# A fused RWKV layer and gated MLP on one core: the order of instructions in time mixing, at the head of the first unit and at stage heads is redone

## The chip, the cores and the metric

One Trainium2 chip, one core. The metric is the device time of one launch in microseconds (us), the median of several runs. All engines are told apart: TensorE (PE, its weight loads PEld), VectorE (DVE), ScalarE (ACT), GpSimd (POOL), and SyncE (SP), which here only issues DMAs. Each engine works through its own list of instructions in order; semaphores tie the lists together.

## The reference

```python
x  = x0 = (1, 2048, 512) tokens;  x = layernorm(x0)            # T = 2048, H = 512
h  = LN(x, ln1);  hh = shift(h)                                 # time mixing
k, v, r = ((h*m + hh*(1-m)) @ W.T for m, W in ((mk,Wk),(mv,Wv),(mr,Wr)))
wkv = (e1*0 + exp(ww-p)*v) / (e1*0 + exp(ww-p))                 # ww = tm_first + k, p = max(-1e38, ww)
x  = x + (sigmoid(r) * wkv) @ Wo.T
h  = LN(x, ln2);  hh = shift(h)                                 # channel mixing
kv = silu((h*cm_mk + hh*(1-cm_mk)) @ Wkey.T) @ Wval.T           # 512 -> 2048 -> 512
x  = x + sigmoid((h*cm_mr + hh*(1-cm_mr)) @ Wcr.T) * kv
x  = x0 + x                                                     # around the attention part
g, up = split(layernorm(x) @ w_gate_up.T);  x = x + (silu(g) * up) @ w_down.T   # 512 -> 2 x 2048 -> 512
```

## The kernel before

**Numbers.** Every matrix product is done in three passes: an operand is split into a high part (fp32r, rounded by an ACT copy) and a low part (the rest, a subtraction on POOL or DVE), and PE multiplies high by high, high by low, and low by high. `..._hi` names the ACT copy, `..._lo` the subtraction.

**Time mixing.** The 2048 tokens are four blocks `b` of 512. For each block PE transposes the normalised tokens into banks A0 to A3 (`norm1`), and ACT, DVE, ACT and POOL turn each of four tiles into an operand: `rest_of` (ACT, L731: the shifted part), `mix` (DVE, L1080 and L1082), `operand_hi` (ACT, L720), `operand_lo` (POOL, L1405). These tiles go through `made`, a ring of four, so a new `rest_of` waits for the POOL subtraction of the tile four places before it. PE then runs, in this order, `receptance(b)`, `output(b-1)`, `key(b)`, `value(b)`, each 48 matmuls of 128x512 on banks B0 to B3. A bank comes free when the sigmoid of the receptance was taken (`receptance_gate`, ACT L748), when DVE added the output to the residual (`output`, L1140), after the exponentials (`wkv_weight`) or after `gated_value` (DVE, L1128). Weights come by SP's DMAs into `landed` and are split by `matrix_hi` (ACT L715) and `matrix_lo` (POOL L1393 or DVE L1107).

**Channel mixing's preparation.** `norm2`, `mix("cr", b)` and `mix_ck(b)` make the operands; PE runs `channel_receptance(b)`; ACT takes its sigmoids (L799), which also free the banks. `x_added(b)` is a POOL DMA that adds the input onto the residual in place; SP then stores the block (`keep_x1`, L380), and after it, in SP's order, `keep_raw(1)`, `keep_gate(2)`, `load_quart(1)`, `keep_gate(3)`, `load_tall(0)`.

**Units.** The two MLPs run as 48 units of a seven-product scheme (Strassen's form) in four stages, starting at units 0, 8, 16 and 32. Units 0 to 15 are key units (0 to 7 and 8 to 15: two pairs of blocks), 16 to 47 gate units. The left operands of a unit come from `quart` (a 0.5 MB DMA, `load_quart`), completed by `sums(u)` on DVE (L1161 to L1166) and split by `unit_left_hi` (ACT L811, L814) and `unit_left_lo` (POOL L1426); the seven right operands of a stage (`combo`: B11, T3, T2, B21, T1, B22, T4) are made by `right_sums`, `make_t2`, `make_t4` (DVE L1203) and split by `combo_hi_of` (ACT L841) and `combo_lo_of` (DVE L1189). The second matmul's right operand is `right` (`unit_right_hi`, L824, and `unit_right_lo`, L1443). Each unit on PE is: products X(B11), V(T3), output tiles of the unit before (`some(0)`), Y(T2), X(B21), tiles, Y(T1) (which waits for `seed`, DVE L1266), tiles, Z(T4), Y(B22) (which waits for `sum_v`, DVE L1270), tiles. `norm3(j)`, at four units, transposes block j for the last MLP into the banks of the output tiles, and ACT copies them out (L880). Silu is taken at L855 and L867.

The order is written out by hand for each engine, in the four engine programs and in their `unit(u)`.

## Time and profile before

| | |
|---|---|
| median of 3 runs | 1101.29 us (1101.24 to 1101.83) |
| the profiled execution: its own time, and its span | 1100.64 us, 1098.8 us |
| PE busy, share of the span | 1060.4 us, 97% |
| DVE, ACT, POOL busy | 633.2, 485.9, 537.9 us |
| chain that ended last | PE 83%, DVE 8%, ACT 3%, POOL 3% |

The span runs from the first to the last instruction. Busy PE time counts a matmul from its start to its modelled end, so matmuls that run at half clock or overlap count as busy too; what is left open between the rows is idle time, and each idle stretch is put down to the instruction that released it.

### The profile page before, as it was taken

The page shows a single profiled execution, that of the slowest core. Times are in us where ns is not written, and L with a number is a line of the kernel's source. Part 1 is how long each engine was busy: PE and PEld are TensorE (multiplying, and loading weights), DVE is VectorE, ACT ScalarE, POOL GpSimd, SP SyncE. Part 2 cuts the span into 40 slices and gives each one's busy share as a digit, 9 for nine tenths or more (in the row PEclk, how much of TensorE's full clock was granted, in tenths as well). Part 3 has the DMA queues.
Part 4 walks back from the last instruction along what each step waited for, and adds up shares of the span by engine and source line. Part 5 has one row for each costly group of instructions (what it writes and reads, how often), then busy time and mean ns, then how long its engine had stood idle before and what let it go on. Part 6 is the DMA issues. An engine that isn't in the chain of part 4 may idle for free.

```text
span 1098.8 us, 13090 instructions
## 1 busy us (share of the span) xinstructions
PE 1060.4 (97%) x4704; PEld 871.4 (79%) x4704; DVE 633.2 (58%) x1106; ACT 485.9 (44%) x807; POOL 537.9 (49%) x451
## 2 busy tenths in 40 slices
PE   5979999999899999999999899999999999999998
PEld 4768888777688888888887788888887888888887
DVE  7866765685344447465449567675658434333334
ACT  6765676855533444433444433334335222222221
POOL 6483652733865553553535656654553323333322
PEclk9989999999999999999999999999999999999999
DMA  8000222257843442653232466575436463444422
GB/s 309 1 1 1 39 39 77 39 211 234 315 144 130 183 172 78 199 186 125 86 106 106 163 225 194 204 229 190 160 129 220 153 205 119 146 153 144 153 78 77
DMA packets 45233, 157.18 MB, mean 143 GB/s; under 512 B 4080, under 2 KB 4208, under 8 KB 40560
## 3 DMA queue, kind: packets, MB, share of 16 engines
q1 hardware_dynamic: 30000, 108.10, 28.1%
q0 software_dynamic: 15168, 48.24, 14.8%
q8 instruction: 37, 0.61, 0.2%
q14 instruction: 28, 0.23, 0.1%
HBM read 97.60 MB, written 58.72 MB: 142 GB/s over the span
## 4 chain that ended last, share of the span: by engine, by line
PE 83%; DVE 8%; ACT 3%; POOL 3%; issue 1%; DMA 1%; SPq 0%; ACTq 0%; DVEq 0%
PE bank L480 15%; PE bank L481 14%; PE bank L482 14%; PE bank L491 13%; PE bank L492 13%; PE bank L493 13%; DVE combo L1189 2%; POOL operand L1405 1%; POOL weights L1393 1%; DVE made L1080 1%; DVE weights L1107 1%; DMA tall_staged<-tall 1%; PE bank L638 1%; DVE resid L1215 1%; PE bank L548 0%
## 5 line engine op out<-in xcount | busy, mean ns | idle before, releaser
L1215 DVE TENSOR_TENSOR resid<-bank,resid 128x512 f32<-128x512 f32 x240 | 165.1, 690 | 243.5 <-PE bank L482 242.3
L491 PE MATMUL bank<-combo,left 128*128 128x512 f32 x672 | 262.8, 391 | 10.2 <-ACT made L855 3.3
L1448 POOL TENSOR_TENSOR inner<-made,inner 128x512 fp32r<-128x512 f32 x128 | 165.9, 1316 | 200.3 <-ACT inner L846 200.3
L493 PE MATMUL bank<-combo,left 128*128 128x512 f32 x672 | 262.0, 390 | 0.0
L492 PE MATMUL bank<-combo,left 128*128 128x512 f32 x672 | 262.0, 390 | 0.0
L480 PE MATMUL bank<-right,inner 128*128 128x512 f32 x512 | 200.0, 391 | 2.8 <-ACT raw L880 2.7
L482 PE MATMUL bank<-right,inner 128*128 128x512 f32 x512 | 199.2, 389 | 0.0
L481 PE MATMUL bank<-right,inner 128*128 128x512 f32 x512 | 199.2, 389 | 0.0
L1426 POOL TENSOR_TENSOR left<-quart,left 128x512 fp32r<-128x512 f32 x96 | 115.6, 1227 | 102.9 <-ACT left L811 63.3
L491 PEld LDWEIGHTS bank<-combo,left 128*128 128x128 f32 x672 | 126.4, 188 | 40.1 <-issue 7.7
L493 PEld LDWEIGHTS bank<-combo,left 128*128 128x128 f32 x672 | 126.4, 188 | 26.4
L492 PEld LDWEIGHTS bank<-combo,left 128*128 128x128 f32 x672 | 126.4, 188 | 25.8
L1443 POOL TENSOR_TENSOR right<-tall_staged,right 128x512 fp32r<-128x512 f32 x64 | 82.8, 1303 | 67.4 <-ACT right L824 67.4
L480 PEld LDWEIGHTS bank<-right,inner 128*128 128x128 f32 x512 | 96.2, 188 | 24.2 <-ACT raw L880 3.7
L482 PEld LDWEIGHTS bank<-right,inner 128*128 128x128 f32 x512 | 96.1, 188 | 20.1
L481 PEld LDWEIGHTS bank<-right,inner 128*128 128x128 f32 x512 | 96.3, 188 | 19.8
L1405 POOL TENSOR_TENSOR operand<-made,operand 128x512 fp32r<-128x512 f32 x64 | 84.9, 1424 | 44.2 <-ACT operand L720 44.2
L867 ACT ACTIVATE made<-bank 128x512 f32<-128x512 f32 x64 | 38.1, 595 | 153.9 <-PE bank L493 153.9
L1280 DVE TENSOR_TENSOR made<-bank,made 128x512 f32<-128x512 f32 x64 | 44.2, 691 | 61.7 <-ACT made L867 41.1
L846 ACT ACTIVATE inner<-made 128x512 fp32r<-128x512 f32 x128 | 77.2, 628 | 2.7 <-ACT made L855 0.4
L855 ACT ACTIVATE made<-bank 128x512 f32<-128x512 f32 x64 | 37.6, 587 | 83.8 <-PE bank L493 83.8
L480 PE MATMUL bank<-operand,weights 128*128 128x512 f32 x176 | 69.3, 394 | 1.8 <-DVE made L1128 1.5
(128 smaller groups left out, 1449.5 us busy)
## 6 DMA issues: line engine op xcount, KB each, us to landing
kept_left<-left SPq DMA_DIRECT2D x24, 1792.0 KB, 8.2
left<-kept_left POOLq DMA_DIRECT2D x24, 1024.0 KB, 7.0
left<-kept_left POOLq DMA_DIRECT2D x24, 768.0 KB, 4.9
tall_staged<-tall SPq DMA_DIRECT2D x64, 256.0 KB, 3.4
quart<-wide SPq DMA_DIRECT2D x24, 512.0 KB, 4.2
raw<-kept SPq DMA_DIRECT2D x32, 256.0 KB, 6.4
landed<-wts SPq DMA_DIRECT2D x20, 256.0 KB, 5.5
resid<-x POOLq DMA_DIRECT2D x4, 1024.0 KB, 9.5
```

The lines of the kernel that those rows point to most:

```text
L480: pe.matmul(acc, left(0), right(0), start=first, stop=False)
L481: pe.matmul(acc, left(0), right(1), start=False, stop=False)
L482: return pe.matmul(acc, left(1), right(0), start=False, stop=last)
L491: pe.matmul(acc[:], hi, combo[:, c, k, 0, :], start=fresh and k == 0, stop=False, skip_group_check=True)
L492: pe.matmul(acc[:], hi, combo[:, c, k, 1, :], start=False, stop=False, skip_group_check=True)
L493: mm = pe.matmul(acc[:], lo, combo[:, c, k, 0, :], start=False, stop=k == 1, skip_group_check=True)
L846: act.activation(inner[:, h % 4, i, 0, :], made_at(n), ACT.Copy).then_inc(inner_hi, 1)
L1215: dve.tensor_tensor(tile, A[s][:], tile, ALU.add).then_inc(added, 1)
L1405: pool.tensor_tensor(place(kind, b, k, 1), made[:, (n + k) % RING, :], place(kind, b, k, 0).bitcast(F32), ALU.subtract).then_inc(op_lo, 1)
L1426: lo = pool.tensor_tensor(left[u % 2][:, 1, a[0]:a[0] + n, :], quart[:, a[0] + 1:a[0] + 1 + n, :], left[u % 2][:, 0, a[0]:a[0] + n, :].bit ...
L1443: pool.tensor_tensor(right[:, g % 2, i, 1, :], tall_staged[i][:], right[:, g % 2, i, 0, :].bitcast(F32), ALU.subtract).then_inc(right_lo, 1)
L1448: pool.tensor_tensor(inner[:, h % 4, i, 1, :], made_at(n), inner[:, h % 4, i, 0, :].bitcast(F32), ALU.subtract).then_inc(inner_lo, 1)
```

## The change

It changes the order of instructions on each engine. No matrix product is added or removed. By place:

- **Start.** `vec` and `ident` are loaded from ACT's queue instead of SP's. DVE finishes the statistics of one tile before those of the next, and makes its constants after the first tile. ACT takes one Sigmoid of one element at the start, and one Silu before the first unit. POOL waits for all four normalised tiles before its first weight subtraction, and makes the low parts of the value weights (DVE did).
- **Mixes.** In `mixed`, the high part of tile k-2 is taken right after `rest_of` of tile k.
- **Block 1.** The four receptance gates are split, two ahead of the key mix and two behind it. On DVE the statistics of blocks 2 and 3 move to later places, and `mix("v", 0)` ahead of `norm1(1)`. On POOL `norm1(2)` moves behind the low parts of `y`.
- **Before the units.** DVE: `output(3)` ahead of `right_sums(0)`; `mix("cr", 3)` and `mix_ck(3)` ahead of `sums(0)`; `sums(1)` ahead of `unit(0)`. ACT: `mixed("cr", 3)` and `rest_of_ck(3)` ahead of the left high parts of unit 0. POOL: `operand_lo("cr", 3)` ahead of the left low parts of unit 0, with `x_added(3)` still behind those.
- **Units.** `norm3` on PE ahead of X(B21). B22 before T4 in the order in which the operands are made; at stage heads `make_t4` after `seed`, T4's high part after the first silu. `right` of unit 0 is made later, its low parts on DVE. `sums(u+1)` at a stage head comes after `sum_v`.

```diff
-MADE_ORDER = (B11, T3, T2, B21, T1, T4, B22)
+MADE_ORDER = (B11, T3, T2, B21, T1, B22, T4)
@@ sync
-            sp.dma_start(resid[:, 0, 0], x_blocks[0][:, 0, :]).then_inc(x_first[0], 16)
-            sp.dma_start(vec[:], vectors).then_inc(vec_loaded, 16)
-            for n in range(1, SUBS):
+            for n in range(SUBS):
                 sp.dma_start(resid[:, 0, n], x_blocks[0][:, n, :]).then_inc(x_first[n], 16)
-            sp.dma_start(ident[:], identity).then_inc(ident_loaded, 16)
@@ tensor, unit
-                product(X, u, A12, B21, False).then_inc(p2, 1)
                 for j in range(BLOCKS):
                     if u == NORM3_UNIT[j]:
                         norm3(j)
+                product(X, u, A12, B21, False).then_inc(p2, 1)
@@ scalar
             def mixed(kind, b):
-                rest_of(kind, b)
-                mix_hi(kind, b)
+                for k in range(KT):
+                    rest_of(kind, b, k)
+                    if k == 2:
+                        place_free(kind, b)
+                    if k >= 2:
+                        operand_hi(kind, b, k - 2)
+                for k in (KT - 2, KT - 1):
+                    operand_hi(kind, b, k)
@@ scalar, unit
-                    combo_hi_of(stage_of(u), T4)
                     combo_hi_of(stage_of(u), B22)
...
-                if is_key(u):
+                if is_key(u) and u:
                     unit_right_hi(u)
-                if u + 1 in FRESH:
+                spread = u in FIRST[1:]
+                if u + 1 in FRESH and not spread:
                     unit_left_hi(u + 1, 1)
                 act.wait_ge(p2, u + 1)
                 if is_key(u):
                     key_tile(u, 0, X)
+                    if u == 0:
+                        unit_right_hi(u)
                 else:
                     gate_tile(u, 0, X)
+                if stage_start(u) and u:
+                    combo_hi_of(stage_of(u), T4)
+                if not is_key(u):
                     unit_right_hi(u)
+                if u + 1 in FRESH and spread:
+                    unit_left_hi(u + 1, 1)
@@ scalar, program
+            act.dma_start(vec[:], vectors).then_inc(vec_loaded, 16)
+            act.dma_start(ident[:], identity).then_inc(ident_loaded, 16)
+            act.wait_ge(half_set, 1)
+            act.activation(table[:], minus_half[:, 0, 0:1], ACT.Sigmoid).then_inc(table_loaded, 1)
...
                 mix_hi("y", b - 1)
-                mixed("k", b)
-                receptance_gate(b)
+                if b == 1:
+                    receptance_gate(b, range(2))
+                    mixed("k", b)
+                    receptance_gate(b, range(2, KT))
+                else:
+                    mixed("k", b)
+                    receptance_gate(b)
...
             combo_hi_of(0, T2)
+            mixed("cr", 3)
+            rest_of_ck(3)
             unit_left_hi(0, 0)
             unit_left_hi(0, 1)
-            mixed("cr", 3)
-            rest_of_ck(3)
             combo_hi_of(0, B21)
             channel_receptance(2)
...
             channel_receptance(3)
+            act.activation(table[:], minus_half[:, 0, 0:1], ACT.Silu).then_inc(table_loaded, 1)
@@ vector, first_norm1
-                summed(0)
-                for s in range(SUBS):
-                    if s + 1 < SUBS:
-                        summed(s + 1)
-                    if s == 1:
-                        constants()
...
+                summed(0)          # now with bn_aggr and the variance of its tile
+                constants()
+                summed(1)
+                summed(2)
+                normed(0)
+                summed(3)
+                for s in range(1, SUBS):
+                    normed(s)
@@ vector, unit
                     combo_lo_of(stage_of(u), T1)
-                    make_t4(stage_of(u))
                 some(0)
                 seed(u)
                 if stage_start(u) and u:
-                    combo_lo_of(stage_of(u), T4)
+                    make_t4(stage_of(u))
+                    combo_lo_of(stage_of(u), B22)
...
-                if u + 1 in FRESH:
+                if u + 1 in FRESH and not stage_start(u):
                     sums(u + 1)
...
                 some(1)
+                if stage_start(u) and u:
+                    combo_lo_of(stage_of(u), T4)
                 sum_v(u)
-                if stage_start(u) and u:
-                    combo_lo_of(stage_of(u), B22)
+                if u == 0:
+                    first_chunk_right_lo()
+                if stage_start(u) and u and u + 1 in FRESH:
+                    sums(u + 1)
@@ vector, program
             norm1_stats(1)
-            matrix_lo(ITEM_V)
+            mix("v", 0)
             norm1(1)
-            mix("v", 0)
             last_token(0, 0)
             wkv_weight(0)
-            norm1_stats(2)
-            for b in range(2):
-                back_to_first(b)
             mix("r", 1)
             for b in range(1, BLOCKS):
                 gated_value(b - 1)
+                if b == 1:
+                    norm1_stats(2)
+                    back_to_first(0)
+                    back_to_first(1)
                 mix("k", b)
...
+                output(b - 1)
                 if b == 1:
                     norm1_stats(3)
-                output(b - 1)
...
             mix_ck(2)
+            output(BLOCKS - 1)
             right_sums(0)
-            output(BLOCKS - 1)
             norm2_stats(BLOCKS - 1)
...
             combo_lo_of(0, T3)
+            mix("cr", 3)
+            mix_ck(3)
             sums(0)
             combo_lo_of(0, T2)
-            mix("cr", 3)
-            mix_ck(3)
...
+            combo_lo_of(0, B22)
             combo_lo_of(0, T4)
-            combo_lo_of(0, B22)
+            sums(1)
             for u in range(UNITS):
                 unit(u)
@@ gpsimd, program
             first_norm1()
+            pool.wait_ge(z1_ready, SUBS)
             matrix_lo(ITEM_R, range(KT - 1))
             operand_lo("r", 0)
             operand_lo("k", 0)
+            matrix_lo(ITEM_V, range(3))
             norm1(1)
+            matrix_lo(ITEM_V, range(3, KT))
             operand_lo("v", 0)
-            norm1(2)
             operand_lo("r", 1)
             matrix_lo(ITEM_O)
             for b in range(1, BLOCKS):
                 operand_lo("y", b - 1)
+                if b == 1:
+                    norm1(2)
...
             norm(2 * BLOCKS - 1)
+            operand_lo("cr", 3)
             unit_left_lo(0, 0)
             unit_left_lo(0, 1)
             x_added(BLOCKS - 1)
-            operand_lo("cr", 3)
```

## Rows read from the trace of the kernel before

**Rows 1.** The page, busy time and share of the span by engine.
```profile
PE 1060.4 (97%) x4704; PEld 871.4 (79%) x4704; DVE 633.2 (58%) x1106; ACT 485.9 (44%) x807; POOL 537.9 (49%) x451
```
**Rows 2.** Waits of PE: who waited for whom; us in total, times, longest.
```profile
PE bank L480 <- ACT held L748: 5.7, 1, 5.7
PE bank L491 <- ACT made L855: 3.3, 2, 2.6
PE bank L491 <- DVE combo L1189: 3.1, 2, 2.8
...
PE bank L480 <- ACT raw L880: 2.7, 4, 0.7
PE bank L491 <- DVE bank L1266: 2.5, 2, 1.7
PE bank L480 <- DVE resid L1140: 2.1, 1, 2.1
PE bank L480 <- DVE made L1128: 1.5, 1, 1.5
```
**Rows 3.** Windows: stretch, length, busy time of each engine, clock, DMA.
```profile
60.00:80.00 20.00, 14.32 (x51) 11.27 (x50) 13.93 (x35) 13.40 (x21) 15.93 (x14) 0.83 0.00 1
...
900.00:1000.00 100.00, 100.00 (x443) 82.81 (x442) 36.71 (x53) 27.36 (x48) 35.68 (x34) 1.00 0.45 145
```
**Rows 4.** Timeline of the start: start, length, engine, line, operation, idle before.
```profile
5.17 0.69 DVE L1016 BATCH_NORM_STATS2 moments<-resid 128x6 f32<-128x512 f32 x1 [1.23 <-DMA resid<-x]
...
10.23 2.15 DVE L1050 TENSOR_SCALAR resid<-resid,stats,rstd 128x512 f32<-128x512 f32 x2 [0.25 <-POOL rstd L1411]
...
13.01 2.78 ACT L731 ACTIVATE made<-bank,vec,rest_g 128x511 f32<-128x511 f32 x4 [1.66 <-PE bank L556]
...
16.45 0.76 PE L512 MATMUL bank<-operand,weights 128*128 128x512 f32 x1 [2.90 <-ACT operand L720]
```
**Rows 5.** Timeline of block 1, from its key mix to its first output.
```profile
64.12 0.78 ACT L731 ACTIVATE made<-bank,vec,rest_g 128x511 f32<-128x511 f32 x1 [4.84 <-POOL operand L1405]
...
69.45 5.55 DVE L1050 TENSOR_SCALAR resid<-resid,stats,rstd 128x512 f32<-128x512 f32 x4
...
70.72 1.28 ACT L748 ACT_TABLE_LOAD   x1
...
72.66 0.79 PE L480 MATMUL bank<-weights,operand 128*128 128x512 f32 x1 [5.68 <-ACT held L748]
...
79.86 2.46 DVE L1035 BATCH_NORM_STATS2 moments<-resid 128x6 f32<-128x512 f32 x4
...
82.78 2.06 DVE L1140 SCALAR_TENSOR_TENSOR resid<-resid,back,bank 128x512 f32<-128x512 f32 x3
```
**Rows 6.** Timeline from the last `norm2` to the first output tile, all engines.
```profile
237.46 1.92 DVE L1154 TENSOR_SCALAR held<-resid,stats,rstd 128x512 f32<-128x512 f32 x4 [1.05 <-DMA kept<-held]
...
242.01 1.14 ACT L841 ACTIVATE combo<-held 128x512 fp32r<-128x512 f32 x2
...
243.97 4.86 POOL L1426 TENSOR_TENSOR left<-quart,left 128x512 fp32r<-128x512 f32 x4 [7.27 <-ACT left L811]
...
248.78 1.29 POOL L1399 DMA_DIRECT2D resid<-x  x1
...
249.47 2.79 ACT L740 ACTIVATE held<-bank,vec,rest_g 128x511 f32<-128x511 f32 x4
...
258.34 0.32 SPq L380 DMA_DIRECT2D kept<-resid  x1
...
269.12 0.70 DVE L1266 TENSOR_TENSOR bank<-bank,e 128x512 f32<-128x512 f32 x1 [7.89 <-PE bank L493]
...
270.76 0.42 DVE L1161 TENSOR_TENSOR quart<-quart 128x256 f32<-128x256 f32 x1 [0.93 <-DMA quart<-wide]
...
282.15 0.50 PE L480 MATMUL bank<-right,inner 128*128 128x512 f32 x1
```
**Rows 7.** Timeline of unit 16, DVE: the making of T4.
```profile
598.32 1.28 DVE L1203 TENSOR_TENSOR raw<-raw 128x512 f32<-128x512 f32 x2
```

More of the change, by code:

```diff
@@ L227, in build @@
         minus_half = sb("minus_half", [P, 2, SUBS])
+        table = sb("table", [P, 1])
         TILE = 4 * BT
@@ L720, in operand_hi, with rest_of @@
                 act.activation(place(kind, b, k, 0), made[:, n % RING, :], ACT.Copy).then_inc(op_hi, 1)
[L722 removed]
+            def rest_of(kind, b, k):
                 n, m = operand_at(kind, b), MIXES[kind]
                 transposed, beta = (t2_psum, 3) if kind == "cr" else (t1_psum, 1)
[L726 to L732 removed]
+                act.wait_ge(transposed, KT * b + k + 1)
+                if n + k >= RING:
+                    act.wait_ge(op_lo, n + k - RING + 1)
+                    act.wait_ge(op_hi, n + k - RING + 1)
+                act.activation(made_at(n + k)[:, 1:BT], A[k][:, 0:BT - 1], ACT.Identity,
+                               bias=vec[:, beta, k:k + 1], scale=rest_g[:, m, k:k + 1]).then_inc(rest_part, 1)
             def rest_of_ck(b):
@@ L741, in rest_of_ck, with receptance_gate @@
                                    scale=rest_g[:, MIXES["ck"], k:k + 1]).then_inc(ck_rest, 1)
-            def receptance_gate(b):
+            def receptance_gate(b, tiles=range(KT)):
                 if b >= 2:
                     act.wait_ge(op_made, operand_at("y", b - 2) + KT)
-                for j in range(KT):
+                for j in tiles:
                     act.wait_ge(r_psum, KT * b + j + 1)
@@ L1184, in right_sums, with first_chunk_right_lo @@
                                       ALU.subtract).then_inc(t_made, 1)
+            def first_chunk_right_lo():
+                for i in range(2):
+                    dve.wait_ge(right_hi, i + 1)
+                    dve.tensor_tensor(right[:, 0, i, 1, :], tall_staged[i][:], right[:, 0, i, 0, :].bitcast(F32),
+                                      ALU.subtract).then_inc(first_right_lo, 1)
             def combo_lo_of(stage, c):
@@ L1464, in unit @@
                     unit_left_lo(u + 1, 0)
-                if is_key(u):
+                if is_key(u) and u:
                     unit_right_lo(u)
```

30 lines of the change are left out of this document (13 added, 17 removed).

## The prediction

> **What bounds the kernel now.** I read the page's busy times, then PE's waits, then windows for the clock, then the timelines around each long wait. PE is busy 97% of the span [rows 1], so it is the bound, and no edit here removes a matmul. All there is to win is PE's idle time and its stretches at half clock. At full clock a 128x512 matmul takes 100 us / 443 = 0.226 us [rows 3]. The waits of PE [rows 2] name nearly everything: the block 1 receptance gates (5.7), the first silu tiles (3.3), T4's and B22's low parts at stage heads (3.1), the copies of `norm3` (2.7, in four places), the `seed` of unit 16 and 32 (2.5), the last output's residual (2.1), `gated_value` (1.5), and the 16.45 us before the first product [rows 4]. In 60 to 80 us the granted clock is 0.83 [rows 3]: it was at the lower level, 1.2 GHz, for 6.8 us around the 5.7 us wait, and matmuls there stood 0.43 us apart. The change touches each of these places. The questions are which waits truly end and what is late next.
>
> **Start.** Before, DVE sat 1.23 us for the second tile of x [rows 4], with its first tile's statistics still unfinished behind it. From a statistic's start to its variances takes 0.93 us, a normalising 0.45, the constants 0.7. In the new order, from x0 at 3.3: variances 4.2, constants 4.9, tile 1 to 5.9, tile 2 to 6.8, normalise one, tile 3 to 8.2, and three more, the last behind POOL's 0.8 us power: 9.6, against 12.4 now (10.23 + 2.15, half of it beside POOL's weight subtractions, which now wait). That is 2.8 us. The interleaved mix gives the first high part after three `rest_of` (0.69 apart, [rows 4]: 2.78 for four) rather than four, 0.6 more, and DVE's subtraction of the last weight row takes 0.2 back: 3.2. The two table loads cost nothing: the first stands where ACT is idle, and the one taken away was before an idle ACT. Bounds: 2.0 (x lands no earlier and the subtraction of R's rows holds the mix) and 3.8. I take 3.3 with a former 0.2 wait at the first gate.
>
> The trace has the four x issues and `vec` 0.45 us apart on SP, and the second x landing 3.5 us after its issue. Moving `vec` away, I let x land up to 0.5 us earlier. The Trainium skill (DMA: Bandwidth & Descriptors, Issuing engines are not separate DMA queues) says that issuing from more engines only saves the issuer's time, since all run on the same 16 DMA engines. By that x1 lands at 5.2 as before and the sum is 0.3 us smaller.
>
> **Blocks 0 and 1.** Everything up to 55 us is fed by ACT, DVE and POOL lists that get shorter: the value weights' low parts leave DVE (2.5 us), the statistics of block 2 (2.9) leave the place ahead of `mix("r", 1)`. So r1's low parts, 5.0 us on POOL, end about 49.7, just before PE is through with `value(0)` (50.1). The wait on `gated_value` and the one behind it (1.5 + 0.3, 2.1 in matmul starts) go.
>
> Then the 5.7 us wait. ACT had r's gates behind the whole key mix, whose `rest_of` waited 4.84 us for POOL's low parts of y [rows 5], and the mix ended at 70.7; a table load of 1.28 and a gate followed [rows 5]. PE had ended at 66.6. In the new order gates 0 and 1 follow the receptance tiles (about 53 and 56), so PE goes from `receptance(1)` (ends 61.0) into `output(0)`; gates 2 and 3 come after the mix, about 63, wanted at 66.5. The wait goes, 5.8 us, and with it the low clock: `output(0)` took 13.8 us and takes 48 x 0.226 = 10.9. Together 8.7.
>
> What is late next is DVE. PE wants the first residual of block 0 when `output(0)` is through, 71.9. DVE went from the start of `norm1(2)`, 69.45, to it at 82.78, 13.3 us with 2.9 us of statistics that now come later [rows 5]: 10.4. It starts that norm when POOL has done y's low parts and the power, 61.4; so 71.8, plus 0.7: a new wait of 0.6 (between 0 and 3). Blocks 2 and 3 show no PE wait, and their chains hang on PE's progress: nothing. Sum so far: 3.3 + 2.1 + 8.7 - 0.6 = 13.5 us.
>
> **From the last output to unit 1: where it is given back.** I keep here the times of before, so 13.5 is still to be subtracted. `output(3)` ahead of `right_sums` lets PE go on at 228.1 instead of 230.3 (2.2). But `norm2(3)` still waits for a DMA and ends at 239.4 [rows 6], so little of that is left. The weight lies in `x_added(3)`. POOL issued it 9.4 us after that norm, at 248.78, right behind the low parts of unit 0 [rows 6]. They are now behind the last mixes. Follow: T2 made at 240.6, its high part 1.14, then mix and `rest_of_ck`. ACT's same work ended at 252.3 (249.47 + 2.79), started 1.4 later and with 1.7 us of left copies inside it: so 249.2 to 249.5. DVE's `mix_ck` ends 1.3 later, 250.8; `sums(0)` 1.3 us alone, up to 3.3 beside POOL; the second left copy 1.05; POOL's low parts half of 4.86 [rows 6]: 255.7 to 257.6, 7 to 9 us late. Now SP is in order: `keep_x1(3)` waits for this DMA, 9.56 us after its issue, and behind it stand 3 MB of stores and `load_quart(1)`, whose quarters came 12.42 us after that [rows 6]: 277.7 to 279.6 instead of 270.76. And DVE now has `sums(1)` ahead of all of unit 0. So `seed(0)` waits: 2.5 us of sums (as before, to 273.3) and 0.7. It was done at 269.8 [rows 6] and will be at 281.0 to 282.9; PE stands idle ahead of Y(T1) some 9 us. A second wait in there, `channel_receptance(3)` for its first bank (the gates come after the left copies: 255 or 257 against PE's 252.2), is covered by it.
>
> After it, unit 0 runs free: three products and two of unit 1, 30 matmuls, 6.8 us, without the waits for silu, because its tiles and the right operands are ready (the silu table is loaded, 1.28 saved, not needed). An idle stretch as long as that was followed by half clock for 6.0 us at 72.66 [rows 5] and for 3 us at the 2.8 us wait: I add 2.2 us. First output tile: 282.0 + 6.8 + 2.2 = 291.0, against 282.15 [rows 6]. The part costs 8.8 us instead of bringing the 7 (2.2 + 4.8 of unit 0's waits) that its edits could. Bounds: -3 (the quarters arrive with x's DMA as before) to +12.
>
> For `sums(0)` beside POOL the trace has the norm of block 2 at 1.39 us an operation beside POOL and the one at 237.46 at 0.48 [rows 5, 6]. The Trainium skill (SBUF — State Buffer, SBUF: two separate sides) calls the port shared by VectorE and GpSimd an exclusive lock for a whole instruction. The trace agrees, and it speaks for the late end, 282.9; with free ports it is 281.0. I took the middle.
>
> **Stage heads and norm3.** Unit 16: DVE has T1's low part at 598.3 [rows 7]. Without `make_t4` first, the tile and `seed` are through at 599.75, PE wants it at 599.87: the 0.83 goes. Then `make_t4`, B22's low part, a tile, T4's: 604.4; PE wants Z(T4) at 602.6, a new wait of 1.8. `sum_v` is ready before Y(B22), which starts at 605.8, not 608.05, and without the half clock behind a 2.8 us wait (1.5). Unit 17 waits 0.2 for its left low parts. 3.6 us. Unit 32 likewise: 1.7 goes, 1.45 comes at Z(T4), 0.3 goes: Y(B22) from 854.7 to 853.75, 0.9. Unit 8 has no wait. `norm3` before X(B21): six matmuls, 1.36 us, cover ACT's first copy; 0.7 and a matmul's refill each, 4 x 0.78 = 3.1. The sums behind z3 are a unit old by then, so nothing new. Together 7.6; bounds 4 and 8.
>
> **The sum.** 13.5 - 8.8 + 7.6 = 12.3 us off the profiled span of 1098.8: 1086.5. That execution's own time is 1100.64, 1.8 more, which makes 1088.3; the median of the runs is 0.65 above it, and I forecast 1089.0 us.
>
> **Rivals.**
> *The quarters aren't late* (the DMA chain is shorter than I think, or SP's wait ends early). For it: x's addition takes 9.6 us and half of that could be queueing. Against: three earlier ones took 9.1 to 9.5 with idle DMA engines. Then the middle part gains 3 instead of losing 8.8: 1077.
> *The gate gain turns into waits on DVE.* `output(0)` on DVE stands behind a norm at 1.39 us an operation. If POOL's y and k1 parts slip by 3 us and the start brings 2.0, PE waits 3 to 4 more at `key(1)` and loses its clock: 1089 + 1.3 + 3.4 + 2 = 1096. Against it: POOL has 5 us less of waiting there than before.
> *It doesn't do what it says*: T4 and gate orders change nothing and unit 0 loses as forecast: 3.3 + 2.1 - 8.8 + 3.1, within 0.3 of nothing: 1101.
> *Slower.* One mechanism: the late quarters carry on. Behind `quart(1)` SP has the raw reloads (2 MB), 1.75 MB of left stores and the tall tiles before `quart(2)`, which came 6.8 us after unit 1's first tile and now would come about 8.0 after it. DVE's order is the same in units 1 to 7: it takes no output tile before `sums(u+1)`. If the quarters come over 11 us after the first tile, each of seven units waits 3 us or more: 1089 + 21 = 1110. Against: 2.8 MB per unit needs 9 us of 20.4.
>
> **How the numbers follow.** Forecast 0.56; quarters not late 0.17; DVE waits 0.14; nothing 0.06; slower 0.07. The range 1077.5 to 1096.5 leaves out the last two and a little more. Within 0.2%, 2.2 us, of 1101.3 counts as no change, about what can be told apart here. Faster: 0.87, same 0.06, slower 0.07.
>
> **What would show it.** Right: first product near 13.2 us; PE without idle from `receptance(1)` into `output(0)` and clock 1.00 in 50 to 80; POOL's `x_added(3)` some 16 to 18 us after the last norm2 and one PE wait of 8 to 10 us on `seed` (L1266's counterpart) with DVE idle for quart; Z(T4) waiting under 2 us at unit 16; no wait on the copies of `norm3`. Wrong: a PE wait at `key(1)` over 3 us; unit 0 without a long wait; PE waits for left operands in units 2 to 7.

## The result, and the profile after

| | before | after |
|---|---|---|
| median (range, runs) | 1101.26 us (1100.63 to 1101.88, 6) | 1096.2 us (1094.17 to 1097.89, 6) |
| profiled execution: time, span | 1100.64, 1098.8 | 1094.17, 1092.4 |

The ratio is 0.9953, with a 95% interval of 0.994 to 0.9966. The change makes the kernel 5.1 us faster; 1089.0 was forecast, 12.3 faster, in a range of 1077.5 to 1096.5. The profiled execution of the changed kernel is the fastest of its six, so its trace shows 6.4 us, more than the medians do. The measured time lies inside the range, but the gain is less than half of what was forecast.

Waits of PE in the changed kernel, as in [rows 2]:

```profile
PE bank L491 <- DVE bank L1300: 6.3, 2, 5.6
PE bank L480 <- ACT raw L811: 3.7, 1, 3.7
PE bank L491 <- DVE combo L1223: 3.1, 2, 1.9
PE bank L548 <- issue: 2.5, 1, 2.5
...
PE bank L480 <- DVE resid L1168: 1.9, 1, 1.9
PE bank L480 <- ACT held L750: 0.7, 1, 0.7
```

The receptance gate (5.7), the first silu tiles (3.3), the copies of `norm3` (2.7), the residual (2.1) and `gated_value` (1.5) are gone from the list. In their place stand the `seed` of unit 0 (5.6), `channel_receptance(3)` (3.7), the transposes of `norm1(1)` (2.5) and `key(1)` (1.9).

Two landmarks of PE cut the span in three. The last matmul of `output(3)` starts at 227.82 us before and at 219.66 after, and one takes 0.23; the first output tile starts at 282.15 before [rows 6] and at 282.90 after.

| stretch | before | after | change | forecast |
|---|---|---|---|---|
| to the end of `output(3)` | 228.05 | 219.9 | -8.15 | -13.5 |
| from there to the first output tile | 54.1 | 63.0 | +8.9 | +8.8 |
| from there to the end | 816.65 | 809.5 | -7.15 | -7.6 |

So the changed kernel was 8.15 us ahead, lost all of it and 0.75 more ahead of its first output tile, and won the rest at the `norm3` places and stage heads. The timeline of the start and of blocks 0 and 1 after, which answers to [rows 4, 5]:

```profile
3.58 0.69 DVE L1045 BATCH_NORM_STATS2 moments<-resid 128x6 f32<-128x512 f32 x1 [3.58 <-DMA resid<-x]
...
9.01 1.67 DVE L1078 TENSOR_SCALAR resid<-resid,stats,rstd 128x512 f32<-128x512 f32 x3
9.17 0.93 POOL L1450 TENSOR_TENSOR rstd<-var_eps,minus_half 128x2 f32<-128x2 f32 x1 [0.59 <-DVE var_eps L1035]
9.60 2.78 PE L556 MATMUL bank<-ident,resid 128*128 128x128 f32 x12 [0.34 <-DVE resid L1078]
...
14.66 0.47 PE L512 MATMUL bank<-operand,weights 128*128 128x512 f32 x1 [2.28 <-ACT operand L723]
...
34.03 5.53 DVE L1078 TENSOR_SCALAR resid<-resid,stats,rstd 128x512 f32<-128x512 f32 x4
...
34.95 5.73 POOL L1444 TENSOR_TENSOR operand<-made,operand 128x512 fp32r<-128x512 f32 x4
...
41.17 1.94 PE L548 MATMUL bank<-ident,resid 128*128 128x128 f32 x16 [2.53 <-issue]
...
66.15 5.60 POOL L1444 TENSOR_TENSOR operand<-made,operand 128x512 fp32r<-128x512 f32 x4
66.29 5.75 DVE L1078 TENSOR_SCALAR resid<-resid,stats,rstd 128x512 f32<-128x512 f32 x4
66.94 1.07 ACT L750 ACTIVATE held<-bank 128x512 f32<-128x512 f32 x2
...
76.89 2.70 DVE L1168 SCALAR_TENSOR_TENSOR resid<-resid,back,bank 128x512 f32<-128x512 f32 x4
...
77.67 0.50 PE L480 MATMUL bank<-operand,weights 128*128 128x512 f32 x1 [1.90 <-DVE resid L1168]
```

The first three gates at 57.41, 59.49 and 66.94 are ahead of PE, which goes from `receptance(1)` into `output(0)` without a stop. But the normalisations of blocks 1 and 2 (34.03 and 66.29) both lie beside POOL's low parts and take 1.4 us an operation, and a PE wait stands behind each. Before, that was so for block 2 alone (69.45 in [rows 5]). The clock of that stretch is at its upper level again, against 0.83 in [rows 3]:

```profile
60.00:80.00 20.00, 18.10 (x80) 14.69 (x79) 19.09 (x42) 11.38 (x19) 16.76 (x13) 1.00 0.00 0
```

The timeline from the last `norm2` to the first output tile, after, which answers to [rows 6]:

```profile
230.03 1.92 DVE L1182 TENSOR_SCALAR held<-resid,stats,rstd 128x512 f32<-128x512 f32 x4 [1.88 <-DMA kept<-held]
...
247.06 2.96 POOL L1465 TENSOR_TENSOR left<-quart,left 128x512 fp32r<-128x512 f32 x2 [2.25 <-ACT left L826]
...
248.56 0.79 PE L480 MATMUL bank<-weights,last_cr 128*128 128x512 f32 x1 [3.67 <-ACT raw L811]
...
249.96 1.31 POOL L1438 DMA_DIRECT2D resid<-x  x1
...
259.28 0.32 SPq L381 DMA_DIRECT2D kept<-resid  x1
...
261.14 1.18 SPq L402 DMA_DIRECT2D quart<-wide  x1
...
270.65 0.43 DVE L1189 TENSOR_TENSOR quart<-quart 128x256 f32<-128x256 f32 x1 [15.14 <-DMA quart<-wide]
...
273.07 0.69 DVE L1300 TENSOR_TENSOR bank<-bank,e 128x512 f32<-128x512 f32 x1
...
273.81 0.80 PE L491 MATMUL bank<-combo,left 128*128 128x512 f32 x1 [5.58 <-DVE bank L1300]
...
282.90 0.39 PE L480 MATMUL bank<-right,inner 128*128 128x512 f32 x1
```

It reads as one chain: the left low parts end, `x_added(3)` is issued, SP waits 9.3 us for it, the quarters are loaded behind the store and land 11.4 us after it, DVE, idle for 15.1 us, makes `sums(1)`, then the `seed`, and PE goes on. At the two long waits the clock falls:

```profile
230.00:260.00 30.00, 25.29 (x107) 20.32 (x106) 22.70 (x40) 18.50 (x32) 11.41 (x9) 0.89 0.41 117
260.00:290.00 30.00, 24.42 (x98) 19.39 (x97) 8.81 (x15) 13.46 (x22) 10.03 (x9) 0.89 0.99 375
```

### The profile page after: what moved, and what is told of

Same layout as the page of the kernel before. It is cut to its first block, busy times and chain, and to the rows that moved or that the text cites. A ratio compares the mean times of both kernels' runs of the same rounds, so it can differ in the third digit from the quotient of the medians.

```text
span 1092.4 us, 13092 instructions
## 1 busy us (share of the span) xinstructions
PE 1058.2 (97%) x4704; PEld 872.0 (80%) x4704; DVE 637.6 (58%) x1104; ACT 484.8 (44%) x808; POOL 540.2 (49%) x453
## 4 chain that ended last, share of the span: by engine, by line
PE 79%; DVE 10%; POOL 5%; ACT 3%; DMA 2%; issue 1%; SPq 0%; ACTq 0%; DVEq 0%; POOLq 0%
PE bank L491 13%; PE bank L493 13%; PE bank L492 13%; PE bank L480 13%; PE bank L481 13%; PE bank L482 13%; POOL operand L1444 3%; DVE combo L1223 2%; POOL weights L1432 1%; DVE resid L1078 1%; DVE made L1108 1%; DMA quart<-wide 1%; DMA kept<-held 1%; DVE moments L1063 1%; PE bank L641 1%
## 5 line engine op out<-in xcount | busy, mean ns | idle before, releaser
L1482 POOL TENSOR_TENSOR right<-tall_staged,right 128x512 fp32r<-128x512 f32 x62 | 80.5, 1307 | 59.2 <-ACT right L836 59.2
```

The lines of the kernel that those rows point to most:

```text
L1482: pool.tensor_tensor(right[:, g % 2, i, 1, :], tall_staged[i][:], right[:, g % 2, i, 0, :].bitcast(F32), ALU.subtract).then_inc(right_lo, 1)
```

## The experiments

Each was timed beside the kernel before, which had medians of 1101.0 to 1101.3 us there. Differences of about 1 us between kernels lie within the spread of their runs.

**Where the middle's 8.9 us come from.** One line of POOL's list is moved:

```diff
             norm(2 * BLOCKS - 1)
+            x_added(BLOCKS - 1)
             operand_lo("cr", 3)
             unit_left_lo(0, 0)
             unit_left_lo(0, 1)
-            x_added(BLOCKS - 1)
```

> The changed kernel with x_added(3) issued by POOL right after the last norm's power, ahead of operand_lo(cr, 3) and the left low parts of unit 0. Theory (the quarters of unit 1 are hostage to this DMA through SP's order): its issue moves from 249.96 to about 232, keep_x1(3) from 259.3 to about 242, load_quart(1) is then held only by keep_gate(2) and goes near 250, lands by 257 instead of 270.65; the 5.6 us wait of PE on seed in unit 0 and the half clock behind it go: 7 to 8 us less than the changed kernel, about 1088.5 us; the 3.7 us wait at channel_receptance(3) stays. Rival (the DMA engines' load delays the quarters, whatever the order): the quarters still land near 270, the wait on seed stays over 4 us, time 1095 to 1097.

Measured: 1086.84 us (1085.44 to 1087.92), ratio 0.9871 (0.9858 to 0.9885), 9.4 less than the changed kernel; 7 to 8 was expected. The two profiled executions differ by 6.25 us, all of it ahead of the first output tile (282.90, then 276.66); the rest of the 9.4 is in no trace. Its timeline:

```profile
234.12 1.32 POOL L1438 DMA_DIRECT2D resid<-x  x1 [4.26 <-DVE held L1182]
...
244.03 0.32 SPq L381 DMA_DIRECT2D kept<-resid  x1
...
251.85 0.32 SPq L385 DMA_DIRECT2D kept<-raw  x1
252.29 0.36 SPq L402 DMA_DIRECT2D quart<-wide  x1
...
257.93 0.43 DVE L1189 TENSOR_TENSOR quart<-quart 128x256 f32<-128x256 f32 x1 [0.57 <-DMA quart<-wide]
...
268.68 0.70 DVE L1300 TENSOR_TENSOR bank<-bank,e 128x512 f32<-128x512 f32 x1 [9.19 <-PE bank L493]
...
276.66 0.39 PE L480 MATMUL bank<-right,inner 128*128 128x512 f32 x1
```

`x_added` is issued 15.8 us earlier, the quarters land 12.7 us earlier although SP now waits for `keep_gate(2)` (251.85) between, and the `seed` waits for PE instead of PE for it. The late addition was the cause. The 3.7 us wait at `channel_receptance(3)` stays, as expected.

The rival cause was DVE's order, `sums(1)` ahead of the `seed`. In the changed kernel alone:

```diff
-                if u + 1 in FRESH and not stage_start(u):
+                if u + 1 in FRESH and not (stage_start(u) and u):
                     sums(u + 1)
...
             combo_lo_of(0, T4)
-            sums(1)
```

> The changed kernel with sums(1) on DVE back behind the seed inside unit(0), its place before the change. PE's Y(T1) waits 5.58 us at 273.81 in the changed kernel, for the seed, which waits for the last quart's load, which was issued late. Theory A, that POOL's late x_added and SP's store are the cause: the load lands at 270.6 all the same, the stall stays as long or moves two products on, and the time is within 1 us of 1096.2. Theory B, that the place of sums(1) ahead of the seed on DVE holds the seed: the 5.58 us go and the time is near 1091.

Measured: 1095.07 us (1092.7 to 1096.87), 1.1 less. The waits of PE have

```profile
PE bank L491 <- DVE bank L1304: 4.0, 1, 4.0
```

where L1304 is `sum_v`: the stall moved two products on, to the next instruction of DVE behind `sums(1)`. Theory A holds in the main: where `sums(1)` stands mostly decides who waits for the late load, and is worth 1.1 us by the medians and 1.8 at the first output tile (281.12 against 282.90).

**What splitting the gates is worth.** The split in block 1 is undone, all four gates behind the key mix.

```diff
-                if b == 1:
-                    receptance_gate(b, range(2))
-                    mixed("k", b)
-                    receptance_gate(b, range(2, KT))
-                else:
-                    mixed("k", b)
-                    receptance_gate(b)
+                mixed("k", b)
+                receptance_gate(b)
```

> The changed kernel with block 1's four receptance gates again behind the whole key mix. Theory (the split removed a real wait): PE waits about 4 us at the first tile of output(0), from 64.7 to near 69, perhaps with some us of half clock; the 1.9 us wait at key(1) goes, since DVE is ready by 77.7; net 3 to 5 us slower than the changed kernel, about 1100 us. Rival (DVE's chain to the first residual bounds block 1 and the split only moved the wait): key(1) starts within 1 us of 77.7 as now, time 1095 to 1097.

Measured: 1099.11 us (1097.44 to 1100.84), 2.9 more than the changed kernel. `output(0)` starts at 69.19 behind a wait of 2.57, with half clock behind it, and `key(1)` doesn't wait:

```profile
69.19 0.69 PE L480 MATMUL bank<-weights,operand 128*128 128x512 f32 x1 [2.57 <-ACT held L750]
```

So of the 5.7 us wait before, more than half went with what was moved ahead of it (POOL's low parts of y end at 67.77 before and at 64.60 after), and the split removed the rest, less the 1.9 us that `key(1)` then waits.

**Is `norm1(1)` on the path?** The value weights' low parts go back to DVE, and `norm1(1)` ahead of `mix("v", 0)`:

```diff
             norm1_stats(1)
+            matrix_lo(ITEM_V)
+            norm1(1)
             mix("v", 0)
-            norm1(1)
@@ gpsimd, program
-            matrix_lo(ITEM_V, range(3))
             norm1(1)
-            matrix_lo(ITEM_V, range(3, KT))
```

> The changed kernel with block 0's value part as before: DVE makes the value weights' low parts, then norm1(1), then mix(v, 0), and POOL does the power of norm1(1) at once. Theory (the norm's four operations ran beside POOL at 1.38 us each and so the edges came late): they take about 0.48 us each again, the last edge column comes near 39.0 instead of 41.1, PE's wait ahead of the transposes of block 1 falls from 2.5 to 0.7 us or less, 1 to 2 us faster than the changed kernel, about 1094.5 us. Rival (the wait follows PE's earlier start, whatever the order): it stays at 2 us or more and the time is 1096 or above.

Measured: 1095.21 us (1094.22 to 1098.1), 1.0 less, within the spread. The four normalisations take 1.91 us together, not 5.53, PE's transposes start at 39.11, and yet:

```profile
39.11 1.07 PE L548 MATMUL bank<-ident,resid 128*128 128x128 f32 x8 [0.49 <-issue]
...
42.22 0.50 PE L480 MATMUL bank<-operand,weights 128*128 128x512 f32 x1 [1.17 <-DVE held L1148]
...
77.46 0.80 PE L480 MATMUL bank<-operand,weights 128*128 128x512 f32 x1 [2.30 <-DVE resid L1168]
```

PE comes to `key(1)` earlier and waits there longer, and starts it 0.2 us earlier than in the changed kernel (77.67). The two waits are in series: the second absorbs what the first gives back. What sets the second is a chain that the order of block 0 hardly moves. ACT begins the receptance mix of block 1 at 46.82 us in the changed kernel and at 46.59 here, and POOL's low parts of y end at 64.60 and 64.36.

The other way round, on top of the kernel with `x_added(3)` first, `norm1(2)` goes behind `output(0)` on DVE:

```diff
-                if b + 1 < BLOCKS:
+                if b == 2:
                     norm1(b + 1)
...
                 output(b - 1)
+                if b == 1:
+                    norm1(b + 1)
+                    back_to_first(b + 1)
```

> a1_x_added_first with, in block 1, DVE's norm1(2) and its back factors moved from between the key and the value mix to behind output(0). Theory (the four norm operations beside POOL's low parts, 5.75 us, make the first residual late and PE wait at key(1)): the residual is ready when PE ends output(0), near 75.6 us, the 2.8 us wait (1.9 in the changed kernel) and the 3.4 us stretch at half clock behind it go, the norm takes 1.9 us in its new place, 2.5 to 4.5 us less than a1: 1083.5 us. Rival (DVE has no room in block 1: the wait moves on to the transposes of norm1(2) or to value(1)): PE waits 2 us or more between 80 and 100 us, time 1086 to 1087.

Measured: 1086.92 us (1084.69 to 1087.41), as without it (1086.84), where 2.5 to 4.5 less was expected. The wait at `key(1)` is gone, and in the traces PE is 3.2 us ahead of the kernel under it behind `key(1)`, but 0.6 behind the gates of block 2. No such wait stands in that kernel; the gates cost 0.7 in the changed one and 1.7 here:

```profile
PE bank L480 <- ACT held L750: 1.7, 1, 1.7
```

**SP's order and `channel_receptance(2)`.** On top of that one, SP stores `keep_gate(0)` ahead of `load_quart(0)`, and ACT takes `channel_receptance(2)` between the two left copies of unit 0:

```diff
             keep_x1(0)
+            keep_gate(0)
             load_quart(0)
             keep_x1(1)
-            keep_gate(0)
...
             unit_left_hi(0, 0)
+            channel_receptance(2)
             unit_left_hi(0, 1)
             combo_hi_of(0, B21)
-            channel_receptance(2)
```

> c1 with two more moves: SP issues keep_gate(0) right after keep_x1(0), ahead of load_quart(0) and keep_x1(1), and ACT takes channel_receptance(2) ahead of the second left copy of unit 0. Theory (norm2(3) waits for that store, 1.5 us on PE, and channel_receptance(3) waits for sigmoids that stand behind DVE's sums, 3.7 us and half clock behind it): norm2(3) on DVE follows its statistics by 1.5 us, both PE waits go, 5 to 8 us less than c1, about 1077 us. Rival (POOL's low parts of cr(3) or the seven right operands are late next): a new PE wait of 2 us or more between 245 and 275 us, time 1080 or above.

Measured: 1080.18 us (1077.92 to 1081.34), 6.7 less. The waits on `norm2(3)` (1.3) and `channel_receptance(3)` (3.7) and the half clock behind them are gone; the first output tile starts at 268.87 instead of 276.11. The two edits weren't tried apart.

**Block 0 again, with the absorbing wait gone.** The edit of block 0 from above, on top of the last kernel:

> The best version so far (x_added first, DVE's norm1(2) behind output(0), the gate's store first, channel_receptance(2) earlier; 1080.2 us), and the four low parts of V's matrix in block 0 on DVE again with norm1(1) ahead of mix(v, 0). In that version PE waits 4.02 us at 42.53 for norm1(1), whose four DVE normalizations take 1.38 us each beside the POOL low parts. Theory A, that this wait is worth what it lasts once nothing later in the chain absorbs it: the wait falls to about 1.7 us (0.49 + 1.17, as in the run with block 0 alone as before) and the time by 2.0 to 2.5, to 1078. Theory B, that another chain (POOL's mixes, the gate of block 2 with its 1.65 us) ends later anyhow: the wait at 42.5 goes, the waits at 77 or 115 grow by as much, and the time stays at 1080 within 0.7.

Measured: 1077.65 us (1077.51 to 1079.13), 2.5 less. The edit that brought 1.0 or nothing in the changed kernel brings 2.5 here, as theory A has it: no wait at `key(1)` is left to take it back. Part of it can have another cause. The two kernels before this one have the changed kernel's instructions up to `norm1(1)`, but in their traces DVE begins it at 35.14 and 35.21, not at 34.03, because the second of two small variance steps is slow beside POOL's weight subtractions:

```profile
30.82 1.33 DVE L1035 TENSOR_SCALAR var_eps<-stats 128x4 f32<-128x4 f32 x1
```

It took 0.16 us in the changed kernel, where only the first step was slow (1.00). With the value weights on DVE again both take 0.17, and the mix of block 1 begins at 46.56, against 48.18 in the kernel under this one and 46.82 in the changed one. How the 2.5 divides isn't shown.

**The gates split in blocks 2 and 3 too**, on top of that:

```diff
-                if b == 1:
-                    receptance_gate(b, range(2))
-                    mixed("k", b)
-                    receptance_gate(b, range(2, KT))
-                else:
-                    mixed("k", b)
-                    receptance_gate(b)
+                receptance_gate(b, range(2))
+                mixed("k", b)
+                receptance_gate(b, range(2, KT))
```

> The kernel of the run before it, and the gate copies of ACT split around the mix of k in every block instead of block 1 alone. The wait of PE's L480 for the gate's operand (1.65 us at 115.18 in the version without it) should be gone in block 2. Theory A, that the wait is on the path: 1.5 us less than the kernel of the run before it, about 1077. Theory B, that in blocks 2 and 3 key and value are then late instead, since two gate copies stand ahead of the mix: the wait goes to L480 of key(2) or key(3), time within 0.7 us of it or up to 1 us more.

Measured: 1076.41 us (1075.53 to 1077.26), ratio to the kernel before 0.9771 (0.9758 to 0.9783): 1.2 less than the kernel under it, close to theory A, and 19.8 less than the changed kernel. The first output tile is 1.9 us earlier (266.18, then 264.26). This is the fastest version. Behind the start its largest wait of PE is

```profile
PE bank L491 <- DVE combo L1219: 3.1, 2, 1.9
```

at the stage heads, and where the changed kernel lost most PE is busy throughout, with its clock at the upper level:

```profile
230.00:260.00 30.00, 30.00 (x134) 24.54 (x133) 21.77 (x40) 24.39 (x41) 14.14 (x12) 1.00 0.82 255
```

**The start.** `vec` and `ident` go back to SP's queue in the changed kernel:

```diff
-            for n in range(SUBS):
+            sp.dma_start(resid[:, 0, 0], x_blocks[0][:, 0, :]).then_inc(x_first[0], 16)
+            sp.dma_start(vec[:], vectors).then_inc(vec_loaded, 16)
+            for n in range(1, SUBS):
                 sp.dma_start(resid[:, 0, n], x_blocks[0][:, n, :]).then_inc(x_first[n], 16)
+            sp.dma_start(ident[:], identity).then_inc(ident_loaded, 16)
...
-            act.dma_start(vec[:], vectors).then_inc(vec_loaded, 16)
-            act.dma_start(ident[:], identity).then_inc(ident_loaded, 16)
```

> The changed kernel with vec and ident loaded from SP's queue again. Theory (two queues bring the second tile of x earlier, so that DVE goes on without a wait): x's tiles 1 to 3 come 0.5 us later, vec later too, DVE's constants and statistics wait, the first product is at 15.2 to 15.6 instead of 14.66 us; what follows absorbs part, since key(1) waits for DVE: time equal or 0.5 us more than the changed kernel, 1096 to 1097. Rival (all run on the same DMA engines, only the issue time moves): first product within 0.2 us of 14.66.

Measured: 1095.99 us (1093.98 to 1098.44), no difference. Its first statistics:

```profile
3.24 0.69 DVE L1046 BATCH_NORM_STATS2 moments<-resid 128x6 f32<-128x512 f32 x1 [3.24 <-DMA resid<-x]
...
5.28 0.69 DVE L1046 BATCH_NORM_STATS2 moments<-resid 128x6 f32<-128x512 f32 x1 [0.18 <-DMA resid<-x]
```

With one queue x's first tile lands 0.34 us earlier than with two (3.24, 3.58), and the first product starts at 14.59 against 14.66: the second queue buys nothing. By the Trainium skill (DMA: Bandwidth & Descriptors, Issuing engines are not separate DMA queues) all issuing engines feed the same DMA engines and a second issuer saves only its own issue time. The runs agree.

The interleaved mix is undone, in all blocks:

```diff
                     rest_of(kind, b, k)
-                    if k == 2:
-                        place_free(kind, b)
-                    if k >= 2:
-                        operand_hi(kind, b, k - 2)
-                for k in (KT - 2, KT - 1):
-                    operand_hi(kind, b, k)
+                mix_hi(kind, b)
```

> The changed kernel with one part of it undone: a mix is again finished in all its tiles on ACT before the first of its high parts, in every block (the high parts are no longer two tiles behind). Theory: only the first mix of r bears on the path, where the first high part comes two ACT instructions later (0.6 us); first product at 15.2 instead of 14.66, time 1096.5 to 1097.0 against 1096.2. Rival: POOL's and DVE's low parts take their turn from the high parts in block 1 too, so that the wait of key(1) (1.90 us) grows by the same 0.6 or more, and the time is 1098.

Measured: 1098.64 us (1097.77 to 1100.99), 2.4 more. The first product starts at 15.24, 0.58 later, as both said; but the rival is right, for the low parts of y end 0.8 us later, and the norm and `key(1)` with them:

```profile
67.11 6.58 DVE L1073 TENSOR_SCALAR resid<-resid,stats,rstd 128x512 f32<-128x512 f32 x4
...
79.33 0.50 PE L480 MATMUL bank<-operand,weights 128*128 128x512 f32 x1 [3.39 <-DVE resid L1163]
```

**`norm3` and the stage heads alone.** Two kernels start from the kernel before. In the first only `norm3` moves ahead of X(B21):

```diff
-                product(X, u, A12, B21, False).then_inc(p2, 1)
                 for j in range(BLOCKS):
                     if u == NORM3_UNIT[j]:
                         norm3(j)
+                product(X, u, A12, B21, False).then_inc(p2, 1)
```

> The kernel before with one edit: norm3 on PE ahead of the product X(B21). Theory: the four waits on ACT's copies of norm3 (0.7 us each, with the refill 0.78) go and nothing comes in their place: 3.1 us less than before, 1098.2 us. Rival (the silu of X comes 1.9 us later in those units and PE waits for it in the next one): no change, 1101 us.

Measured: 1097.78 us (1095.14 to 1099.05), 3.4 less than before; forecast 3.1.

The second has the edits of unit heads alone, T4 and B22 exchanged with them (cut to its core):

```diff
-MADE_ORDER = (B11, T3, T2, B21, T1, T4, B22)
+MADE_ORDER = (B11, T3, T2, B21, T1, B22, T4)
...
-                    make_t4(stage_of(u))
                 some(0)
...
-                    combo_lo_of(stage_of(u), T4)
+                    make_t4(stage_of(u))
+                    combo_lo_of(stage_of(u), B22)
...
+                    combo_lo_of(stage_of(u), T4)
+                sum_v(u)
+                if stage_start(u) and u and u + 1 in FRESH:
+                    sums(u + 1)
```

> The kernel before with the edits of the stage heads alone: B22 made before T4, make_t4 after seed, T4's high part after the first silu, the sums behind sum_v. Theory (waits of 0.83, 2.78 and the half clock at unit 16, 1.7 and 0.3 at unit 32 go, 1.2 and 1.95 on T4's low part come): 3.5 to 4.5 us less than before, about 1097 us. Rival (only the wait's name changes and the half clock stays): 1100 us.

Measured: 1099.14 us (1097.27 to 1099.38), 2.2 less than before (1101.33 beside it), where 3.5 to 4.5 was expected. In its trace unit 16 waits 0.76 and 1.19 us at full clock; in the changed kernel 0.72 (at 599.38) and 1.17, and unit 32 waits 1.95:

```profile
603.58 0.50 PE L491 MATMUL bank<-combo,left 128*128 128x512 f32 x1 [1.17 <-DVE combo L1223]
...
846.81 0.50 PE L491 MATMUL bank<-combo,left 128*128 128x512 f32 x1 [1.95 <-DVE combo L1223]
```

The profiled execution (1097.51) lies 1.6 under that median. Compare the start of the same matmul in it and in the trace of before: unit 16 brings 2.85 us and unit 32 brings 0.35, together 3.2, where the prediction had 3.6 and 0.9. At unit 32 the new wait of 1.95 nearly equals the 1.7 and 0.3 that go; at unit 16 most of the 0.83 stays. Ahead of unit 16 the two traces are level (0.1), although this one has two stretches with matmuls 0.43 us apart, from 230.7 and from 278.7, behind waits of 2.05 and 2.45 us that didn't slow the matmuls in the trace of before (2.09 and 2.56).

## Why the prediction was wrong in size

**The middle, +8.8, was right** in size and in its main chain (measured +8.9). `x_added(3)` came 18.0 us after `norm2(3)` had ended (16 to 18 forecast), SP's store 9.3 behind it (9.56), the quarters 11.4 behind that (12.42). The split differs: 5.6 us at the `seed` where 9 was forecast, behind 3.7 at `channel_receptance(3)` and half clock. Both are covered by the late `seed`, as the prediction said of the wait. In the kernel with the gates whole the same 3.7 us wait has no half clock behind it, and PE waits 8.8 us at the `seed` instead of 5.6. The last experiments show that nearly all of this stall and the waits before it can be had back.

**`norm3` and heads, -7.6, were right in sum** (measured -7.15), with two errors that cancel. All four copies' waits are gone, and by the starts of the same matmuls each place brings 0.97 us, 3.9 in all (3.1 forecast). The heads bring 2.8 at unit 16 (3.6) and 0.3 at unit 32 (0.9). Z(T4) waits 1.2 at unit 16 (1.8 forecast) and 1.95 at unit 32 (1.45), and a wait of 0.72 stays ahead of it at unit 16.

**The step that failed** is the early sum, "3.3 + 2.1 + 8.7 - 0.6 = 13.5 us". It measured 8.15. Under it lies one assumption: that everything up to 55 us is fed by ACT, DVE and POOL lists that get shorter, so that r1's low parts end about 49.7. They ended at 54.60, 4.9 us later, and 57.80 before. In the changed kernel:

```profile
42.06 0.60 ACT L760 ACTIVATE e<-bank 128x512 f32<-128x512 f32 x1 [3.64 <-DVE held L1145]
...
46.82 1.45 ACT L733 ACTIVATE made<-bank,vec,rest_g 128x511 f32<-128x511 f32 x2
...
49.53 5.07 POOL L1444 TENSOR_TENSOR operand<-made,operand 128x512 fp32r<-128x512 f32 x4 [8.85 <-ACT operand L723]
...
59.55 5.05 POOL L1444 TENSOR_TENSOR operand<-made,operand 128x512 fp32r<-128x512 f32 x4
```

and before:

```profile
46.72 1.44 ACT L731 ACTIVATE made<-bank,vec,rest_g 128x511 f32<-128x511 f32 x2
...
52.77 5.03 POOL L1405 TENSOR_TENSOR operand<-made,operand 128x512 fp32r<-128x512 f32 x4 [0.40 <-ACT operand L720]
```

ACT can't begin the receptance mix of block 1 until it has made the exponentials of block 0's keys, in turns with DVE. DVE's first product of these came at 40.85 before, where it waited for ACT; at 40.99 after, where ACT waited 3.64 us for DVE, busy with `norm1(1)` and the edges; and at 40.73 with block 0 as before. So the mix begins at 46.72, 46.82 and 46.59 us. In the changed kernel DVE's list was not shorter: the value weights left it (2.5 us by the forecast), but `norm1(1)` beside POOL takes 5.53 instead of 1.9, and a small variance step ahead of it 1.00 instead of 0.17. That this chain sets the mix shows in the other traces with this block 0: where DVE begins `norm1(1)` at 32.98 the mix begins at 45.45, and where it begins at 35.14 and 35.21, at 48.14 and 48.18. Only what stands between the mix and its low parts got shorter (6.05 us, then 2.71), which is mainly the statistics. From 49.53 POOL works without a stop through r1's low parts, a weight's and y's, so the 4.9 us come out unchanged at the norm of block 2: 66.29, not 61.4. The terms on PE:

- The start, 3.3: the first product went from 16.45 to 14.66, 1.8. Two things weren't in it: the last norm ended at 10.68, not 9.6, because the third and fourth variances came at 7.43 and 8.95 with POOL's 0.93 us power behind each; and PE's transposes of three tiles come in one stretch, 9.60 to 12.38, which the first `rest_of` (11.88) waited for.
- The waits of `gated_value`, 2.1: gone, as forecast. But block 0's new order was priced at nothing beyond that. With the value weights' low parts on POOL, and `mix("v", 0)` ahead, `norm1(1)` now runs beside POOL at 1.38 us an operation instead of 0.48, and PE waits 2.5, where it didn't wait before.
- The gate and its clock, 8.7: gone, as forecast. Undoing the split alone costs 2.9, so it is not the split by itself.
- `key(1)`, "a new wait of 0.6": it is 1.9. DVE's norm started at 66.29, not 61.4, as shown above, and PE too came later, out of `output(0)` near 75.6 and not at 71.9, so only 1.3 of the 4.9 us shows as wait.
- Block 2, "nothing": 0.7 for its gates.

These add up to 1.8 + 2.1 - 2.5 + 8.7 - 1.9 - 0.7 = 7.5. By the starts of the same matmuls in the two traces, which count the refill behind a wait too, it is 1.80 + 0.35 - 2.74 + 2.65 + 8.76 - 2.13 - 0.99 + 0.46 = 8.16. The 0.35 is in the first product, whose first four matmuls start 0.23 to 0.31 us apart after and 0.43 to 0.56 before. The 0.46 is a last stretch, where a wait of 0.4 ahead of `norm2` is gone.

The price of DVE beside POOL was in my rows (1.39 us an operation in block 2) and I used it for `sums(0)` and `norm1(2)`, but not for `norm1(1)`, where the change itself put POOL's work. These 3.6 us and the 1.5 that the start fell short make 5.1, about the 4.9 by which block 1 was late. The old order gives nothing better, for there DVE has the value weights again: the mix of block 1 begins 0.23 us earlier and `key(1)` 0.2. The Trainium skill (SBUF — State Buffer, SBUF: two separate sides) states that the port which the two engines share is an exclusive lock for a whole instruction; 5.53 us for four operations beside POOL and 1.91 without, in two kernels that differ in block 0 alone, agree with it.

Of the 7.2 us between forecast and median, 5.9 stand in the profiled execution (1094.17 against 1088.3, nearly all in the early sum), and 1.3 are that this execution lies 2.0 under its median where before it lay 0.65 under. In three other kernels with this block 1 `key(1)` waited 2.30, 2.72 and 2.77 us, in two of them with half clock behind it, and in a fourth (the loads on SP) the clock fell already behind a 2.7 us wait at `norm1(1)`. That the usual run of the changed kernel loses its clock in such a place, and the profiled one didn't, fits the 1.3 us but isn't shown.

**The rivals.** "The gate gain turns into waits on DVE" gave 1096, and came nearest: its two conditions held (the start brought 1.8, and POOL's parts slipped by 4.9, more than its 3). It put all 3 to 4 us at `key(1)`; they came as 2.5 at `norm1(1)` and 1.3 there, and the clock loss it counted isn't in the profiled execution. That its time is so close to the median is in part luck. It deserved more than 0.14, as a norm at 1.39 us was already in the trace. Quarters that aren't late did not occur by this change, but with one line moved they gave 1086.8. The units behind `seed(0)` did not wait for their quarters: the slower rival is false.

## What to carry to other kernels

An operation moved from DVE to POOL doesn't shorten DVE's list by its own time if it then slows others there: here both orders of block 0 led to the same mix at 46.6 to 46.8 us. Before a list of POOL is lengthened, see which DVE operations it will now lie beside, and price these at their duration beside POOL, also where no wait stood before. Waits along one chain don't add: an edit that removes one is worth what the next wait on the chain lets through, so the same edit gave 1.0 us or less alone and, with the next wait gone, 2.5 us (part of it perhaps by another cause). Where an in-order queue has a store that waits ahead of a load, the instruction that releases the store belongs at the first place where its data is ready.

## What the runs showed of the hardware

- The same wait of PE is sometimes followed by a stretch at half clock (1.2 GHz) and sometimes not. `key(1)` in block 1: 1.90 and 2.72 us, none; 2.30, 2.77 and 3.39, one each. The residual before unit 0: 2.09, none; 2.05, one. The changed kernel's six runs spread over 3.7 us (1094.17 to 1097.89), the first six of before over 1.3; but the runs of before that were timed beside the experiments spread over 3.0, 2.6 and 4.1 us, so the wide spread isn't the changed kernel's own.
- Very small DVE operations suffer beside POOL as well: in one trace `back`'s 128x4 multiplication took 1.13 us beside POOL's low parts (59.75) and 0.16 without them (72.16). In block 0 one such step, 128x4, took 0.16 us in the changed kernel and 1.33 and 1.34 in two others with the same instructions up to there, and put `norm1(1)` and the mix of block 1 off by 1.1 to 1.4 us.
